# Writing out the sixteen batches of cross attention in place of a loop over pairs

## The chip, the cores and the metric

The kernel runs on one core of a Trainium2 chip. That core has five engines with an instruction stream each: TensorE (PE, matmuls, with its weight loads shown as PEld), VectorE (DVE), ScalarE (ACT), GpSimd (POOL) and SyncE (SP, which only issues DMAs here). They meet only through semaphores. The metric is the device time of one execution in microseconds (us), the median of several runs; lower is better.

## The reference

The model takes x (16 batches x 64 tokens x 256) and a context (16 x 1601 x 192) through six steps, each added to x: cross attention, linear attention, a mixture of experts, a second cross attention with a filter, path attention, and expert-choice experts. The change touches the first alone:

```
def _L0_xattn_ref(x, y, Wq, bq, Wk, bk, Wv, bv, Wo, bo):
    q = _split_heads(x @ Wq + bq)          # 16 heads of 16
    k = _split_heads(y @ Wk + bk)
    v = _split_heads(y @ Wv + bv)
    scores = jnp.einsum('bhqd,bhkd->bhqk', q, k) * scale
    weights = jax.nn.softmax(scores, axis=-1)
    out = jnp.einsum('bhqk,bhkd->bhqd', weights, v)
    out = out.transpose(0, 2, 1, 3).reshape(x.shape[0], x.shape[1], D_ATT)
    return out @ Wo + bo
```

It is called with the layer norm of x and with the context as y. All is in fp32.

## The kernel before

The six steps run one after the other, each in a block of its own in which every engine has its program; the blocks of the other steps have loops of their own. x stays in SBUF.

In `cross_attention` the work goes batch by batch (B = 16, in TILES = 8 pairs, since two batches of 64 tokens fill the 128 partitions). It is a pipeline over two batches: a body for batch n computes its scores, exponentials and weighted sums, and beside that the keys, values and row maxima of batch n + 1. Buffers are double, by h = n mod 2. A body has seven rounds t, each over 256 of the 1601 context rows:

- PE makes the transposed scores of batch n (`scores`, L350), then weighs the values of the round before with its exponentials (`weigh`, L361), then makes a part of the next batch's keys (`keys`, L315) or values (`values`, L322), then direct scores of the next batch for its maximum (`direct`, L331), then another part of keys or values. At the end of a body it spreads the next batch's maximum (`spread_maximum`, L339). The output projection (`project`, L382) comes once in a pair.
- VectorE spreads the queries (L605), subtracts the maximum (L628) and reduces the direct scores (L611, L616).
- ScalarE copies keys and values out of PSUM (L522, L528) and takes exponentials (L536).
- SyncE loads the context of batch b (1.2 MB, L288) when the values of batch b - 2 are made.

Each engine's order is written by hand, and each wait is for a count that grows with the batch. In round 0 of a body, PE's scores stand without a wait of their own ahead of them; in the later rounds they wait for the subtraction and the reduction. On PE, ScalarE and VectorE a helper `batches` (L268) calls the body: batches 0 and 1 are written out, batches 2 to 13 are six passes of a hardware loop whose body holds two batches, and 14 and 15 are written out again. In the loop, n is an expression of the loop's register, and so are the counts waited for and some addresses. SyncE has batches 0 and 1 written out and a loop over the other seven pairs (`first_then_loop`, L31). The engines' loops don't synchronise with each other at their ends; only the semaphores of the work do.

In path attention (`path_attention`) PE runs a loop over the 16 batches as well; its first batch is written out. Its body begins with the matmuls of L2042.

Of the kernel before, what the change touches and what calls it, by code (L numbers as in the profile page):

```python
# [14 lines left out]
B, T, D = 16, 64, 256  # L15
TILES = B * T // P
# [10 lines left out]
def width(c):  # L27
    return P if c < KC - 1 else KLAST


def first_then_loop(eng, count):  # L31

    yield 0
    with eng.Fori(1, count) as i:
        yield i
# [189 lines left out]
def cross_attention(core):  # L225
# [9 lines left out]
    with ExitStack() as stack:  # L235
# [29 lines left out]
        quad = [slice(32 * j, 32 * j + 32) for j in range(4)]  # L265
        block = stack.enter_context(nc.Block())

        def batches(eng, body):  # L268

            body(0, 0, 0, True, False)  # L270
            body(1, 0, 1, False, False)
            with eng.Fori(1, TILES - 1) as i:
                body(2 * i, i, 0, False, False)
                body(2 * i + 1, i, 1, False, False)
            body(B - 2, TILES - 1, 0, False, False)
            body(B - 1, TILES - 1, 1, False, True)

        @block.sync
        def _(sp):
            for dst, name in ((wq, "xa_wq"), (wo, "xa_wo"), (wk, "xa_wk"), (wv, "xa_wv"), (bq, "xa_bq"),  # L280
                              (bk, "xa_bk"), (bv, "xa_bv"), (bo, "xa_bo")):
                sp.dma_start(dst[:], ins[name]).then_inc(w_loaded, 16)
            for i in first_then_loop(sp, TILES):
                for h in range(2):
                    b = 2 * i + h
                    if not isinstance(i, int):
                        sp.wait_ge(v_ps, 7 * (b - 1))
                    sp.dma_start(ctxT[:, h, :, :], ins["ctxT"][ds(b, 1)].rearrange("a k c n -> c (a k) n")  # L288
                                 ).then_inc(ctx_loaded[h], 16)
# [9 lines left out]
        def _(pe):  # L299
# [197 lines left out]
                if not last:  # L497
                    last_maximum(n + 1, 1 - h)

            batches(pe, body)  # L500
            pe.wait_ge(e_done, 7 * B)
            weigh(1, 6)
            pe.wait_ge(oT_ready, 2 * (B - 1))
# [4 lines left out]
        @block.scalar  # L508
        def _(act):
            a_ = nc.scalar.activation  # L510
            ln.scalar(act)
            act.wait_ge(bias_scaled, 1)
            for n in range(2):
                for m in range(KD):
                    act.wait_ge(q_ps, 2 * n + m + 1)
                    a_(qT[:, m, n * 512:(n + 1) * 512], ps[:, 2 * n + m, :], ACT.Identity,
                       bias=bq[:, m:m + 1], scale=DH ** -0.5).then_inc(q_sb, 1)

            def keys_out(b, h, n):
                a, z = PARTS[n // 2]  # L520
                act.wait_ge(k_ps, 8 * b + n + 1)
                a_(kT[:, h, n % 2, a:z], ps[:, KEY_BANK[n], 0:z - a], ACT.Identity, bias=bk[:, n % 2:n % 2 + 1]  # L522
                   ).then_inc(k_sb, 1)

            def values_out(b, h, g):
                w, chunks = width(2 * g), 2 if g < 6 else 1
                act.wait_ge(v_ps, 7 * b + g + 1)
                a_(v[0:w, h, 2 * g:2 * g + chunks].rearrange("p c m d -> p (c m) d")[:, :, 0:16],  # L528
                   ps[0:w, VALUE_BANK[g], 0:chunks * D].rearrange("p (m d) -> p m d", d=16), ACT.Copy).then_inc(v_sb, 1)

            def exponentials(n, h, t):
                w = width(2 * t)
                act.wait_ge(sub_done, 7 * n + t + 1)
                o = probT[0:w, (7 * h + t) % 2].rearrange("p j r c n -> p (j r) c n")
                o = o.rearrange("p u c n -> p (u c n)") if t < 6 else o[:, :, 0, :]
                a_(o, o, ACT.Exp, bias=core.zero[0:w]).then_inc(e_done, 1)  # L536

            def copy_out(b):
                act.wait_ge(pv_done, 7 * b + 7)
                a_(sums_out[:], ps[:, OUT, 0:2 * P], ACT.Copy).then_inc(o_sb, 1)  # L540

            def own_out(b, h):
                act.wait_ge(u_ps, b + 1)
                for e in range(2):
                    a_(oT[:, e, h, :], ps[:, OWN_BANK, e * T:(e + 1) * T], ACT.Identity, bias=bv[:, e:e + 1]).then_inc(oT_ready, 1)

            def spread_out(b):
                act.wait_ge(n_ps, b + 1)
                a_(shift[:].rearrange("p u n -> p (u n)"), ps[:, 5:7, :].rearrange("p b n -> p (b n)"), ACT.Copy
                   ).then_inc(n_sb, 1)  # L550

            def under_shift(b, h, t):
                if t < 4:
                    keys_out(b, h, 2 * t)
                else:
                    values_out(b, h, 2 * (t - 4))

            def under_maximum(b, h, t):
                if t < 4:
                    keys_out(b, h, 2 * t + 1)  # L560
                else:
                    values_out(b, h, 2 * (t - 4) + 1)

            def last_maximum(b, h):
                values_out(b, h, 6)
                spread_out(b)

            for t in range(ROUNDS):
                under_shift(0, 0, t)
                under_maximum(0, 0, t)  # L570
            last_maximum(0, 0)

            def body(n, i, h, first, last):
                for t in range(ROUNDS):
                    if t == 0 and not first:
                        copy_out(n - 1)
                    if t == 3 and not first:
                        own_out(n - 1, 1 - h)
                    if not last:
                        under_shift(n + 1, 1 - h, t)  # L580
                    exponentials(n, h, t)
                    if not last:
                        under_maximum(n + 1, 1 - h, t)
                if not last:
                    last_maximum(n + 1, 1 - h)

            batches(act, body)
            copy_out(B - 1)
            own_out(B - 1, 1)

        @block.vector
        def _(dve):
# [11 lines left out]
            def spread(b, h):  # L604
                v_.tensor_tensor(qb[:, h], qT[:, :, ds(b * T, T)].unsqueeze(2).broadcast_to([P, 2, 2, T]),  # L605
                                 pair_mask[:].unsqueeze(1).unsqueeze(3).broadcast_to([P, 2, 2, T]), ALU.mult).then_inc(qb_ready, 1)

            def reduce(b, n):
                a, z = PARTS[n // 2]
                dve.wait_ge(m_ps, MAXES * b + n + 1)  # L610
                v_.tensor_reduce(part[:, :, n % 2, n // 2], ps[:, 0:4, 0:z - a], AX.X, ALU.max,  # L611
                                 negate=True).then_inc(m_used, 1)

            def maximum(b):
                dve.wait_ge(m_used, MAXES * b + MAXES)
                v_.tensor_reduce(nmax[:], part[:].rearrange("p j r s -> p (j r) s"), AX.X, ALU.min).then_inc(max_step, 1)  # L616

            def subtract(n, h, t, first):

                w, chunks = width(2 * t), 2 if t < 6 else 1  # L620
                dve.wait_ge(s_ps, 7 * n + t + 1)
                if t == 0:
                    dve.wait_ge(n_sb, n + 1)
                if not first or t >= 2:
                    dve.wait_ge(pv_done, 7 * n + t - 1)
                got = ps[0:w, 0:4, :].rearrange("p j (r c n) -> p (j r) c n", r=2, c=2)
                o = probT[0:w, (7 * h + t) % 2].rearrange("p j r c n -> p (j r) c n")
                v_.tensor_tensor(o[:, :, 0:chunks], got[:, :, 0:chunks],  # L628
                                 shift[0:w].unsqueeze(2).broadcast_to([w, 8, chunks, P]), ALU.add).then_inc(sub_done, 1)
# [9 lines left out]
            def add(i):  # L639
                dve.wait_ge(y_ps, i + 1)  # L640
                xt = core.x[:, ds(i, 1), :].rearrange("p a n -> p (a n)")
                v_.tensor_tensor(xt, ps[:, Y_BANK, 0:D], xt, ALU.add).then_inc(x_done, 1)
# [6 lines left out]
            def body(n, i, h, first, last):  # L649
                if not last:  # L650
                    if not first:
                        dve.wait_ge(s_ps, 7 * n)
                    spread(n + 1, 1 - h)
                for t in range(ROUNDS):
                    subtract(n, h, t, first)
                    if not last:
                        reduce(n + 1, t)
                    if t == 1 and not first:
                        normalise(n - 1)
                    if t == 4 and not first and not h:  # L660
                        add(i - 1)
                if not last:
                    reduce(n + 1, 7)
                    maximum(n + 1)

            batches(dve, body)
            normalise(B - 1)
            add(TILES - 1)

# [1942 lines left out]
```

## Time and profile before

| | us |
|---|---|
| median of 3 runs | 3106.34 (3101.46 to 3115.24) |
| the profiled execution, own time | 3107.18 |
| its span, first to last instruction | 3105.4 |
| cross attention's batches in it, about | 76 to 970 |
| PE busy | 2625.1 |
| VectorE busy | 1784.2 |
| ScalarE busy | 1100.4 |
| mean granted clock of PE | 0.915 of full speed |

A row of the timeline is a run of equal instructions with its start, its length, the engine and the line of the code. The list of waits says before which work an engine sat idle and what ended that; "issue" there means that the profile shows nothing that it waited for. The granted clock (PEclk) is 1.00 at full speed and 0.50 at half speed. The DMA queue q8 is one that brings instructions, in packets of 16 KB; q1 brings data.

### The profile page before, as it was taken

What the parts mean: (1) busy time and instruction counts of PE and PEld (TensorE: products, weight loads), DVE (VectorE), ACT (ScalarE), POOL (GpSimd) and SP (SyncE); (2) the same over time, 40 slices, a digit from 0 to 9 for tenths busy, and PEclk for the clock granted to TensorE, in tenths of its full rate; (3) what the DMA queues carried; (4) which work ended last, traced back from release to release, by engine and by line L of the source; (5) the groups of instructions that cost most, each with busy time, mean ns of one, the idle gap of its engine ahead of it and who ended that gap; (6) DMA issues with size and microseconds to landing.
All of it is one profiled execution on the core that took longest, in us unless ns stands there. A gap on an engine that the chain in (4) does not pass through costs nothing. (4 is left out here: it accounts for less than half of the span.)

```text
span 3105.4 us, 80772 instructions
## 1 busy us (share of the span) xinstructions
PE 2625.1 (85%) x34608; PEld 1907.8 (61%) x34608; DVE 1784.2 (57%) x2561; ACT 1100.4 (35%) x1715; POOL 752.6 (24%) x964
## 2 busy tenths in 40 slices
PE   5998988988997899888888868875888888888598
PEld 3565555555564455455655545533888888878487
DVE  4654544545554444399999958158555555655500
ACT  2443433433443111245555531244333323332121
POOL 6900000000000000023333340022556545653200
PEclk9999989999998889999999979987998899899699
DMA  2001001001000011222222210010000000000131
GB/s 72 23 18 33 18 18 34 18 18 34 18 2 22 0 36 35 67 81 82 77 84 74 72 47 1 0 31 4 4 4 3 4 4 4 4 4 3 55 136 41
DMA packets 24546, 99.41 MB, mean 32 GB/s; under 512 B 4825, under 2 KB 9838, under 8 KB 19503
## 3 DMA queue, kind: packets, MB, share of 16 engines
q1 hardware_dynamic: 24238, 94.57, 10.4%
q8 instruction: 284, 4.65, 0.6%
q14 instruction: 24, 0.19, 0.0%
HBM read 93.51 MB, written 1.05 MB: 30 GB/s over the span
## 5 line engine op out<-in xcount | busy, mean ns | idle before, releaser
L611 DVE TENSOR_REDUCE xa_minus_max_parts<-psum 128x4 f32<-128x1600 f32 (+1 forms) x128 | 233.9, 1827 | 220.6 <-PE psum L331 220.6
L628 DVE TENSOR_TENSOR xa_probT<-psum,xa_minus_max_spread 128x2048 f32<-128x2048 f32 (+1 forms) x112 | 239.5, 2139 | 198.1 <-PE psum L350 198.1
L315 PE MATMUL psum<-xa_ctxT,xa_wk 96*128 96x400 f32 (+1 forms) x512 | 217.9, 551 | 2.1 <-DVE xa_qb L605 1.3
L2193 ACT ACTIVATE pa_x<-psum 128x256 f32<-128x256 f32 x256 | 98.1, 383 | 332.0 <-PE psum L2052 316.4
L536 ACT ACTIVATE xa_probT<-xa_probT,zero_column 128x2048 f32<-128x2048 f32 (+1 forms) x112 | 209.4, 1870 | 8.9 <-DVE xa_probT L628 8.9
L322 PE MATMUL psum<-xa_wv,xa_ctxT 96*128 96x256 f32 (+1 forms) x832 | 208.0, 392 | 0.0
L1279 POOL TENSOR_TENSOR tk_exp_all<-tk_exp_all,tk_exp_left 128x577 f32<-128x577 f32 x64 | 120.8, 1888 | 354.5 <-ACT tk_exp_left L1400 354.5
L2017 POOL TENSOR_TENSOR pa_cT<-pa_mt_and_qw,pa_levelT 128x256 f32<-128x256 f32 x256 | 192.3, 784 | 58.6 <-PE psum L2052 58.6
L2271 DVE TENSOR_TENSOR pa_inv_and_invT<-pa_inv_and_invT,psum 128x512 f32<-128x512 f32 x192 | 131.9, 687 | 117.8 <-PE psum L2052 117.6
L716 POOL MEMSET la_v<- 128x512 f32 x1 | 0.5, 524 | 809.9 <-remote 809.9
L350 PE MATMUL psum<-xa_qb,xa_kT 32*128 32x128 f32 (+1 forms) x3328 | 131.8, 295 | 60.8 <-issue 29.2
L322 PEld LDWEIGHTS psum<-xa_wv,xa_ctxT 96*128 96x128 f32 (+1 forms) x832 | 145.7, 185 | 60.7 <-ACT xa_v L528 27.5
L350 PEld LDWEIGHTS psum<-xa_qb,xa_kT 32*128 32x128 f32 (+1 forms) x3328 | 111.5, 194 | 114.7 <-issue 108.8
L1447 DVE MAX8 tk_top<-tk_left 128x8 f32<-128x1601 f32 x96 | 175.1, 1824 | 4.1
L1449 DVE MATCH_REPLACE8 tk_left<-tk_top,tk_left 128x1601 f32<-128x1601 f32 x96 | 173.9, 1811 | 0.0
L2052 PE MATMUL psum<-pa_inv_and_invT,pa_cT 64*64 64x64 f32 x4096 | 144.0, 229 | 28.2 <-DVE pa_prob L2232 24.5
L1352 PE MATMUL psum<-tk_ctx,tk_attnT 128*128 128x192 f32 (+1 forms) x832 | 148.2, 337 | 14.7 <-ACT tk_attnT L1406 14.0
L1332 PE MATMUL psum<-tk_ctxT,tk_qwt 97*128 97x512 f32 (+1 forms) x256 | 128.3, 585 | 36.8 <-ACT tk_ctxT L1422 32.6
L2052 PE MATMUL psum<-pa_inv_and_invT,pa_x 64*64 64x64 f32 x4096 | 157.8, 219 | 0.0
L2052 PEld LDWEIGHTS psum<-pa_inv_and_invT,pa_cT 64*64 64x64 f32 x4096 | 135.2, 143 | 36.3 <-issue 35.7
L1352 PEld LDWEIGHTS psum<-tk_ctx,tk_attnT 128*128 128x128 f32 (+1 forms) x832 | 139.4, 196 | 21.3 <-ACT tk_attnT L1406 21.3
L528 ACT ACTIVATE xa_v<-psum 128x512 f32<-128x512 f32 (+1 forms) x112 | 63.4, 566 | 233.2 <-PE psum L322 233.2
(471 smaller groups left out, 5208.5 us busy)
## 6 DMA issues: line engine op xcount, KB each, us to landing
tk_ctx<-in_ctx SPq DMA_DIRECT2D x16, 1248.0 KB, 5.4
xa_ctxT<-in_ctxT SPq DMA_DIRECT2D x16, 1200.8 KB, 7.4
tk_ctxT<-in_ctxT SPq DMA_DIRECT2D x16, 1200.8 KB
ec_w<-in_ec_w SPq DMA_DIRECT2D x16, 1024.0 KB, 6.8
m_gate_up<-in_m_gate_up SPq DMA_DIRECT2D x17, 256.0 KB, 2.6
m_down<-in_m_down SPq DMA_DIRECT2D x17, 128.0 KB, 2.5
ff_w<-in_ff_w SPq DMA_DIRECT2D x2, 1024.0 KB
x_resident<-in_x SPq DMA_DIRECT2D x1, 1024.0 KB, 4.9
```

The source lines that it names most:

```text
L315: mm = mmul(ps[:, KEY_BANK[n], 0:z - a], wk[:, k, m * P:(m + 1) * P], ctxT[:, h, k, a:z], start=(k == 0), stop=(k == 1))
L322: mm = mmul(ps[0:width(c), VALUE_BANK[g], (c % 2) * D:(c % 2 + 1) * D], ctxT[:, h, k, c * P:c * P + width(c)], wv[:, k, :], start=(k == 0) ...
L350: mm = mmul(ps[0:w, j, (2 * r + c) * P:(2 * r + c + 1) * P], kT[quad[j], h, r, at:at + w], qb[quad[j], h, r, :, :].rearrange("p e t -> p ( ...
L536: a_(o, o, ACT.Exp, bias=core.zero[0:w]).then_inc(e_done, 1)
L611: v_.tensor_reduce(part[:, :, n % 2, n // 2], ps[:, 0:4, 0:z - a], AX.X, ALU.max, negate=True).then_inc(m_used, 1)
L628: v_.tensor_tensor(o[:, :, 0:chunks], got[:, :, 0:chunks], shift[0:w].unsqueeze(2).broadcast_to([w, 8, chunks, P]), ALU.add).then_inc(sub_ ...
L1352: mm = nc.tensor.matmul(flat[:, CCOL:CCOL + C], aT[0:width(c), c, :], ctx[0:width(c), h, c, :], start=(c == KC - 1), stop=(c == 7))
L1447: c.step(nc.vector.max(best, src))
L1449: c.step(nc.vector.match_replace(left[:, u % 2, :], best, src, TAKEN))
L2017: g_.tensor_tensor(cT[:, n % 2, g], mq[:, g, :, 0, :], four(levelT[:, n, :]), ALU.mult).then_inc(level_ready, 1)
L2052: mm = mmul(ps[rows, at, column + j * T:column + (j + 1) * T], left[rows, g, j, :], right[rows, g, j, :], **flags)
L2271: v.tensor_tensor(whole, whole, ps[:, 4 + g, :], ALU.subtract).then_inc(inv_sb, 1)
```

## The change

`batches` is replaced by a plain loop of the program that builds the kernel, so that all sixteen bodies are written out on PE, ScalarE and VectorE, and SyncE's loads likewise. The order of the instructions in a body, the waits, the buffers and the work are the same. The counts and addresses become constants.

```
-        def batches(eng, body):
-
-            body(0, 0, 0, True, False)
-            body(1, 0, 1, False, False)
-            with eng.Fori(1, TILES - 1) as i:
-                body(2 * i, i, 0, False, False)
-                body(2 * i + 1, i, 1, False, False)
-            body(B - 2, TILES - 1, 0, False, False)
-            body(B - 1, TILES - 1, 1, False, True)
+        def batches(body):
+
+            for n in range(B):
+                body(n, n // 2, n % 2, n == 0, n == B - 1)
...
-            for i in first_then_loop(sp, TILES):
+            for i in range(TILES):
                 for h in range(2):
                     b = 2 * i + h
-                    if not isinstance(i, int):
+                    if i:
                         sp.wait_ge(v_ps, 7 * (b - 1))
...
-            batches(pe, body)
+            batches(body)
...
-            batches(act, body)
+            batches(body)
...
-            batches(dve, body)
+            batches(body)
```


## Rows read from the trace of the kernel before

Times are us from the span's start unless marked ns. The waits give us in total, times, longest; a DMA queue row packets, MB, share of the 16 engines. A window's row gives its length, then busy us and count of PE, PEld, DVE, ACT, POOL, then PEclk, DMA share, GB/s. The brackets at the end of a timeline row hold the idle time before it and what released it.

**Rows 1.** the page, busy us (share of the span) x instructions of each engine

```profile
PE 2625.1 (85%) x34608; PEld 1907.8 (61%) x34608; DVE 1784.2 (57%) x2561; ACT 1100.4 (35%) x1715; POOL 752.6 (24%) x964
```

**Rows 2.** who waited for whom, PE, 297 to 885 us: us, times, longest

```profile
PE psum L350 <- issue: 29.2, 5, 6.1
PE psum L350 <- DVE xa_minus_max_parts L611: 15.8, 35, 0.5
```

**Rows 3.** the same view, PE, 184.8 to 291.8 us, whole

```profile
PE psum L350 <- DVE xa_minus_max_parts L611: 3.7, 8, 0.5
PE psum L339 <- DVE xa_minus_max L616: 2.5, 2, 1.3
PE psum L331 <- ACT xa_kT L522: 1.4, 2, 0.7
```

**Rows 4.** timeline (start, us, engine line), PE, boundary of bodies 2 and 3

```profile
237.17 2.02 PE L339 MATMUL psum<-ident,xa_minus_max 128*128 128x128 f32 x16 [1.25 <-DVE xa_minus_max L616]
239.13 1.17 PE L350 MATMUL psum<-xa_qb,xa_kT 32*128 32x128 f32 x32
240.23 0.64 PE L361 MATMUL psum<-xa_probT,xa_v 65*17 65x64 f32 x32
240.80 1.61 PE L315 MATMUL psum<-xa_ctxT,xa_wk 96*128 96x401 f32 x4
243.10 0.96 PE L331 MATMUL psum<-xa_kT,xa_qb 32*128 32x401 f32 x8 [0.69 <-ACT xa_kT L522]
```

**Rows 5.** timeline, all engines, 284 to 302 us, the loop's first jump back

```profile
288.81 0.32 SPq L288 DMA_DIRECT2D xa_ctxT<-in_ctxT  x1
...
289.89 2.02 PE L339 MATMUL psum<-ident,xa_minus_max 128*128 128x128 f32 x16 [1.25 <-DVE xa_minus_max L616]
290.22 0.42 DVE L605 TENSOR_TENSOR xa_qb<-xa_qT,xa_pair_mask 128x256 f32<-128x256 f32 x1 [0.48 <-issue]
...
297.88 2.09 PE L350 MATMUL psum<-xa_qb,xa_kT 32*128 32x128 f32 x32 [5.97 <-issue]
```

**Rows 6.** busy us of each engine, PEclk, DMA by window: straight stretch; behind jump

```profile
88.00:182.00 94.00, 87.65 (x1420) 56.25 (x1407) 57.18 (x32) 40.72 (x45) 67.28 (x75) 1.00 0.06 15
...
297.88:311.84 13.96, 13.27 (x136) 7.82 (x140) 4.56 (x3) 3.46 (x4) 0.00 (x0) 0.50 0.01 2
```

**Rows 7.** the same view for the first, second and last pair of looped bodies

```profile
184.73:291.85 107.12, 99.06 (x1589) 64.05 (x1588) 61.54 (x39) 45.78 (x52) 0.00 (x0) 1.00 0.11 25
297.88:416.73 118.85, 105.49 (x1589) 67.78 (x1589) 61.54 (x39) 45.77 (x52) 0.00 (x0) 0.93 0.10 23
...
770.77:882.91 112.14, 104.59 (x1589) 67.02 (x1589) 61.54 (x39) 44.75 (x51) 0.00 (x0) 0.94 0.06 13
```

**Rows 8.** the same view for body 1, before the loop

```profile
131.93:184.73 52.80, 48.69 (x793) 31.58 (x792) 30.94 (x20) 22.89 (x26) 27.72 (x18) 1.00 0.11 24
```

**Rows 9.** the page, DMA issues: count, KB each, us to landing

```profile
xa_ctxT<-in_ctxT SPq DMA_DIRECT2D x16, 1200.8 KB, 7.4
```

**Rows 10.** DMA queues, instruction packets: 184.73 to 291.85, then 297.88 to 416.73 us

```profile
q8 instruction: 13, 0.21, 0.9%
...
q8 instruction: 14, 0.23, 0.8%
```

**Rows 11.** DMA queues: 288.8 to 294.5, then 294.5 to 297 us

```profile
q1 hardware_dynamic: 178, 1.14, 84.3%
...
q8 instruction: 1, 0.02, 3.3%
```

**Rows 12.** who waited for whom, PE, 2160 to 2880 us

```profile
PE psum L2042 <- issue: 44.9, 14, 3.5
```

**Rows 13.** timeline, SyncE, 232 to 242 us; DMA queues, 242.5 to 245 us

```profile
236.09 0.32 SPq L288 DMA_DIRECT2D xa_ctxT<-in_ctxT  x1
...
q8 instruction: 1, 0.02, 3.0%
```

**Rows 14.** timeline, PE, 79 to 90 us, in body 0

```profile
80.81 1.72 PE L331 MATMUL psum<-xa_kT,xa_qb 32*128 32x401 f32 x8 [0.78 <-ACT xa_kT L522]
```

## Prediction, made before the changed kernel was run

> **What bounds the kernel now.** I read the page first. TensorE (PE) is busy 85% of the span, VectorE 57%, ScalarE 35% [rows 1]. So PE's own stream of instructions sets the pace, and what ends PE's idle times is the question. The list of who waited for whom, for PE from 297 to 885 us, answers it [rows 2]: 29.2 us in 5 waits, up to 6.1 us long, stand at the first score matmul (L350) with no releaser ("issue"), beside 15.8 us in 35 short waits for VectorE's reductions. In the two loop bodies before that (184.8 to 291.8) the "issue" entry is missing altogether; the whole list is three kinds of short waits, 3.7 + 2.5 + 1.4 = 7.6 us [rows 3]. Five is the number of times that a loop of six passes jumps back.
>
> The timeline shows the place. At a boundary between two bodies that are neighbours in the code (237 to 239 us), PE ends the spreading of the maximum (L339), which began at 237.17, and begins the next scores at 239.13, 1.96 us later and with no idle time [rows 4]. At a boundary where the loop jumps back, L339 begins at 289.89 and L350 only at 297.88 [rows 5]: 5.97 us idle. Nothing that this matmul needs is late: the program has no wait before the scores of round 0 and VectorE's last work before it, begun at 290.22 [rows 5], is for the next batch. The other four edges are in the 29.2 us of the list [rows 2].
>
> [...]
>
> **The change, part by part.** (1) The five jumps back go. The cost of a pair of bodies is read as the distance between the first L350 of even batches [rows 5, 7]: with 184.73 and 297.88 the first two, it is 118.85 us from 297.88 to 416.73, and 112.14 for the last pair, from 770.77 to 882.91, which ends without a jump. What a pair takes in straight code is in the trace as well: the first pass is entered without a jump, and its work ends at 289.89 + 1.96 = 291.85, so it takes 291.85 - 184.73 = 107.12 us, at clock 1.00 all through, 99.06 us of it busy [rows 7]. The six passes took 882.91 - 184.73 = 698.18 us, and six straight ones would take 6 x 107.12 = 642.72. The difference is 55.46 us. It splits in the 29.2 us of idle time [rows 2] and a remainder of 26.3 us of slow clock, 5.3 us for each edge. I take both parts as gained: the slow clock stands behind an edge, and in the straight stretches from 88 to 182 and 184.73 to 291.85 it was 1.00 throughout [rows 6, 7], so without the idle time nothing seen here lowers it. What becomes late next is what the straight pair already contains: the waits for VectorE and ScalarE, 7.6 us a pair [rows 3], are inside the 107.12.
>
> (2) The waits and addresses that were computed from the loop's register become constants. Bodies 0, 1, 14 and 15 had constants already. Body 3, with registers, took 52.72 us (from 239.13 [rows 4] to 291.85); body 1, with constants, from 131.93 to 184.73, 52.80 us [rows 8]. So this is worth nothing to within 0.1 us a body, and I take zero; the bounds are -1 and +1 us over twelve bodies. VectorE jumps too, and has an idle time of 0.48 us before its first work behind the jump [rows 5]; that lies under PE's gap and is zero on the path. ScalarE and SyncE jump while they wait for PE anyway. These go at no gain.
>
> (3) SyncE's context transfers keep their order and their waits. Batch b's transfer starts when the values of batch b - 2 are made, and is needed a body (some 53 us) later, against a landing of 7.4 us [rows 9]. Zero.
>
> (4) What is added is code. Ten more bodies lie in line on each engine. Does PE's supply of instructions keep up? The instruction queue of the DMA engines shows it: in the straight pair 13 packets of 16 KB arrive, in a looped pair 14 [rows 10]. The loop's code is brought in anew on every pass, so writing it out brings no more traffic, one packet fewer for each edge. Straight code of this very density (first pass) shows no idle time for it. So zero, with the bounds under the rivals.
>
> Why an edge costs 6 us: the context transfer of 1.2 MB begins at 288.81, just ahead of the jump [rows 5]. From 288.8 to 294.5 only the data queue moves, 178 packets at 84% of the engines; the instruction packet comes in the stretch from 294.5 to 297, and PE starts at 297.88 [rows 11]. In path attention, where nothing is being loaded, PE's idle time at the loop's edges (L2042) is 44.9 us in 14 waits, 3.2 us each [rows 12]. So about 3.2 us are the jump and 2.6 us, the rest of 29.2 / 5 = 5.8, the queueing behind the data. For the sum this doesn't matter, both go; it matters for the first rival.
>
> [...]
>
> The sum: -29.2 - 26.3 = -55.5 us. The profiled execution took 3107.2 us around a span of 3105.4, and the median of the runs shown is 3106.3, so the profile stands 0.8 us above it. 3107.2 - 55.5 = 3051.7 for such an execution, 3050.8 for the median.
>
> **The rivals.** A, slower than before: starved prefetch. In straight code the next instruction packet can also queue behind a context transfer. It seems to: at the boundary of 236 us, where a transfer is issued at 236.09, the next packet of this queue comes in 242.5 to 245 [rows 13]. If PE runs through the block that it holds before that, it idles with 6 us at the worst and then pays the slow clock's 5.3. What protects it is that the stretch under a transfer is thin in instructions: from 236.1 to 243.1 PE runs 16 + 32 + 32 + 4 matmuls [rows 4], each with one weight load, 168 instructions, and a packet of 16 KB carries more: 13 packets serve 1589 matmuls and 1588 loads [rows 7, 10], over 240 in each. The boundary at 236 shows it without idle time. But the straight code meets some ten more transfers, each at a place in its block not sampled so far. Lost at all ten, 8 us each (2.6 of queueing and 5.3 of clock, as above), that is 80 us: 3051 + 80 = 3131. It decides from 5.5 us on average over the ten. Against it speaks that about 70 instructions are to spare; chance 0.04.
>
> B: the later loops move. The code of the following stages begins elsewhere in its 16 KB blocks. If the target of path attention's jump comes to lie near a block's end, PE runs into a second fetch: up to 2 us more at each of 14 edges, since 32 matmuls with their loads take 1.2 to 2.1 us [rows 4, 5] against the 3.2 us of a jump's fetch. 28 us more: 3079. One or two missed prefetches of A are worth as much. It can also go the other way, if fewer of these 14 edges are followed by the slow clock: half a microsecond or so at each with the matmuls of [rows 4, 5], under 10 us in all, 3041. Chance of a loss of 15 to 35 us: 0.09.
>
> C: the idle time goes but the clock doesn't gain. If the clock falls of itself some time in long dense runs, the 26.3 us stay: 3077. For it: in the first written-out body, without a jump, the eight matmuls at 80.81 us take 1.72 us, where those at 243.10 take 0.96, behind an idle time of 0.78 [rows 14, 4]. Against it: 94 and 107 us at 1.00 [rows 6, 7]. Chance 0.04.
>
> D: the gap isn't the jump but the transfer, or the change does nothing to it: 3106. The boundary at 236 us has the same transfer (issued at 236.09) and no gap [rows 13, 4], which nearly excludes it. Chance 0.03.
>
> **How the numbers follow.** Forecast, 3035 to 3066 us: 0.80. B 0.09, C 0.04, D 0.03, A 0.04. Predicted 3051. The range of 8 in 10 reaches down by B's possible gain with the runs' own spread (3040; these went from 3101.5 to 3115.2), and up over the lighter half of B (3070). About 0.5%, or 15.5 us, is what a measurement of this kernel can tell from no change: faster than that are the forecast, B, C: 0.93; I give 0.92 for faster, 0.05 for the same (D, and part of A), and 0.03 for slower.
>
> **What would show it.** PE's wait list should have no "issue" of over 1 us at L350; pairs of bodies should be 107.1 us apart from first to last; granted clock 1.00 from 88 us to the end of cross attention; batch 14's first L350 at 184.7 + 642.7 = 827.4 instead of 882.9 us. The edges in path attention should still stand at about 3.2 us, 14 times. Wrong would be: "issue" idle times of 2 to 6 us on PE at new places, just behind the start of a context transfer (A); longer ones at L2042 (B); slices of clock 0.5 within cross attention with no idle time before them (C).

## The result

The changed kernel takes 3083.99 us (median of 8 runs, 3076.17 to 3096.16) against 3114.82 (3095.28 to 3126.99) for the kernel before: ratio 0.990, with an interval of 0.9875 to 0.9925. It is faster by 31 us, about 1%; the forecast was 55 us, and the range of 3040 to 3070 missed the time. Its profiled execution took 3081.99 us with a span of 3080.4, 25.0 us under the span of before.

The first stage did what was forecast. Three windows of pairs of bodies in the changed kernel, the last one ending at batch 14's first L345 (L350 before); columns as in [rows 6, 7]:

```profile
184.92:292.19 107.27, 99.05 (x1591) 64.13 (x1590) 61.36 (x39) 45.77 (x52) 0.00 (x0) 1.00 0.10 25
292.19:399.46 107.27, 99.05 (x1591) 64.12 (x1590) 61.35 (x39) 45.78 (x52) 0.00 (x0) 1.00 0.11 25
...
721.26:828.53 107.27, 99.05 (x1591) 64.12 (x1590) 61.36 (x39) 45.78 (x52) 0.00 (x0) 1.00 0.08 20
```

Each pair takes 107.27 us at full clock, where looped ones took up to 118.85 [rows 7]. Who waited for whom, PE, 60 to 980 us of the changed kernel, longest in total first:

```profile
PE psum L345 <- DVE xa_minus_max_parts L606: 27.0, 59, 0.5
PE psum L334 <- DVE xa_minus_max L611: 20.0, 16, 1.3
PE psum L326 <- ACT xa_kT L517: 11.7, 15, 0.8
PE psum L164 <- DVE la_ln_xn L155: 5.8, 1, 5.8
```

The 29.2 us without a releaser [rows 2] are gone. The first transposes of linear attention (L164) start at 919.37 us in the changed kernel and at 975.64 before: 56.3 us earlier.

The rest came back later. Two windows of each kernel, linear attention and the stretch of path attention from its first to its last moving matmul; first before, then after:

```profile
975.64:1096.38 120.74, 99.41 (x352) 56.08 (x352) 53.78 (x116) 25.38 (x45) 2.64 (x6) 0.80 0.03 9
2155.60:2821.50 665.90, 575.75 (x16168) 557.25 (x16172) 370.53 (x608) 224.44 (x519) 373.37 (x497) 0.91 0.02 4
```

```profile
919.37:1046.10 126.73, 105.25 (x353) 59.30 (x353) 53.77 (x116) 25.46 (x45) 2.64 (x6) 0.76 0.03 9
2101.70:2793.60 691.90, 603.19 (x16174) 578.68 (x16174) 377.57 (x610) 224.35 (x519) 373.51 (x499) 0.87 0.02 4
```

Path attention's stretch is 26.0 us longer with the same work, at a mean clock of 0.87 in place of 0.91. All of it is busy time, 603.19 us against 575.75; the rest of the stretch, in which PE sits idle, went from 90.2 to 88.7 us. Linear attention is 6.0 us longer, with the same count of work and a lower clock. All other stages together are 0.7 us shorter: 56.3 - 26.0 - 6.0 + 0.7 = 25.0.

In path attention the waits without a releaser rose, and those for VectorE fell. From PE's list for 2095 to 2810 us of the changed kernel (its L2037 is L2042 of [rows 12]), and, last, the line of before that answers its third:

```profile
PE psum L2037 <- issue: 61.9, 25, 4.3
...
PE psum L2047 <- issue: 6.0, 17, 0.6
...
PE psum L2065 <- DVE pa_mt_and_qw L2252: 1.4, 1, 1.4
```

```profile
PE psum L2070 <- DVE pa_mt_and_qw L2257: 16.4, 14, 1.7
```

The first was 44.9 us in 14 waits [rows 12] and is 61.9 in 25; the third was 16.4 us and is 1.4. The timeline of one edge shows one of the eleven extra waits:

```profile
2231.97 2.09 PE L2037 MATMUL psum<-pa_moving,pa_wt 32*128 32x128 f32 x32 [4.29 <-issue]
2233.84 0.65 PE L2037 MATMUL psum<-pa_moving,pa_wbt 32*128 32x128 f32 x7
2235.17 1.86 PE L2037 MATMUL psum<-pa_moving,pa_wbt 32*128 32x128 f32 x25 [0.68 <-issue]
```

PE stops in the middle of a group of equal matmuls, after 32 + 7 = 39 of them, which no semaphore explains. All eleven stand at this matmul. The view of one source line holds the jump itself, on PE's sequencer. Lowest, median and highest duration in ns; first the line of path attention's loop, then that of cross attention's, both before, then path attention's after:

```profile
L2149 PEldq COMPARE_BRANCH  x15: 83/3671/3887, 2234.7 to 2861.3; - x15
```

```profile
L272 PEldq COMPARE_BRANCH  x6: 83/7558/7784, 290.1 to 881.1; - x6
```

```profile
L2144 PEldq COMPARE_BRANCH  x15: 83/4208/4662, 2180.6 to 2832.1; - x15
```

The 83 ns are the last pass, where the jump isn't taken. Path attention's jumps went from 3.67 to 4.21 us though nothing in its loop was edited. What did change is where it lies: ten more bodies of code stand ahead of it. That is rival B, to which the prediction gave 0.09.

### The profile page after: what moved, and what is told of

It is laid out like the page before. It is cut to its first block and busy times, and to the rows that moved or that the text cites. A ratio compares the mean times of both kernels' runs of the same rounds, so it can differ in the third digit from the quotient of the medians.

```text
span 3080.4 us, 79974 instructions
## 1 busy us (share of the span) xinstructions
PE 2628.9 (85%) x34608; PEld 1915.9 (62%) x34608; DVE 1789.2 (58%) x2561; ACT 1100.4 (36%) x1715; POOL 751.2 (24%) x964
## 5 line engine op out<-in xcount | busy, mean ns | idle before, releaser
L310 PE MATMUL psum<-xa_ctxT,xa_wk 96*128 96x400 f32 (+1 forms) x512 | 204.0, 521 | 2.2 <-DVE xa_qb L600 1.3
L2047 PE MATMUL psum<-pa_inv_and_invT,pa_cT 64*64 64x64 f32 x4096 | 142.6, 227 | 19.7 <-DVE pa_prob L2227 16.1
L345 PEld LDWEIGHTS psum<-xa_qb,xa_kT 32*128 32x128 f32 (+1 forms) x3328 | 105.4, 184 | 86.0 <-issue 78.9
L345 PE MATMUL psum<-xa_qb,xa_kT 32*128 32x128 f32 (+1 forms) x3328 | 125.1, 285 | 34.4 <-DVE xa_minus_max_parts L606 27.0
L2047 PEld LDWEIGHTS psum<-pa_inv_and_invT,pa_cT 64*64 64x64 f32 x4096 | 133.8, 142 | 28.0 <-issue 27.4
```

Of the source, the lines that this page charges most:

```text
L310: mm = mmul(ps[:, KEY_BANK[n], 0:z - a], wk[:, k, m * P:(m + 1) * P], ctxT[:, h, k, a:z], start=(k == 0), stop=(k == 1))
L345: mm = mmul(ps[0:w, j, (2 * r + c) * P:(2 * r + c + 1) * P], kT[quad[j], h, r, at:at + w], qb[quad[j], h, r, :, :].rearrange("p e t -> p ( ...
L2047: mm = mmul(ps[rows, at, column + j * T:column + (j + 1) * T], left[rows, g, j, :], right[rows, g, j, :], **flags)
```

## The experiments

Two questions: is it the place of path attention's loop that cost 26 us, and what did the edges in cross attention really cost? PE's code comes in the 16 KB packets of q8. Over the straight code of cross attention in the changed kernel (90 to 880 us) PE runs 256.1 instructions from one packet to the next on average (92 packets), so a fetch block of 16 KB is taken as 256 instructions. A helper of the language places a loop's first instruction at a chosen one of them. "Place s" below means s instructions lie ahead of the target in its block.

**Places 0 and 224, in the changed kernel.**

```
-                with pe.Fori(1, B) as b:
+                with nc.Fori(1, B, engines=bass.OrderedEngineSet([pe.engine]), head_slot={pe.engine: 0}) as b:
```

> The changed kernel, with one edit: PE's loop in path attention is placed so that its first instruction is the first of a 16 KB fetch block (256 instructions); the padding before it is jumped over once. Theory 1 (the loss of 26 us in path attention comes from where the loop now lies in its blocks: about 83 instructions of the block are left behind the jump's target, PE then runs dry, and a prefetch is in flight when it jumps): the second idle time behind each jump goes, the jumps take some 3.6 us instead of 4.2, the stretch from path attention's first moving matmul to the last is back at about 666 us from 692, and the whole at about 3058 us. Theory 2 (the loss has nothing to do with the place, but with the clock after a denser first stage or with this execution): the stretch stays at 692 us and the whole at 3082.

Measured 3062.72 us (3053.97 to 3072.81), ratio 0.9828 (0.9793 to 0.9863). The jumps are back at 3.5 us and no second wait follows one, but the profiled execution, the slowest of the four, had a stretch of 685.6 us. PE's waits without a releaser in that stretch:

```profile
PE psum L2037 <- issue: 45.6, 15, 3.4
...
PE psum L2047 <- issue: 17.9, 30, 1.2
```

The first line is as before the change; the second, the waits within the body, was 2.9 us there. So theory 1 holds for the edges and misses 15 us of waits in the body.

> The changed kernel, with PE's loop in path attention placed 32 instructions before the end of a fetch block. Theory 1 (place): PE runs out after some 16 matmuls behind each of the 14 jumps and waits for 2 to 3 us for the next block, so there are 14 more waits of that size than in the well placed loop; the stretch takes 695 to 720 us and the whole 3085 to 3110 us, no gain over the kernel before. Theory 2 (not the place): 692 us and 3082, as in the changed kernel.

Measured 3102.66 us (3091.31 to 3108.22), ratio 0.9972 (0.9953 to 0.9991): theory 1. The timeline counts the instructions that were left:

```profile
2226.63 1.23 PE L2037 MATMUL psum<-pa_moving,pa_wt 32*128 32x128 f32 x15 [3.56 <-issue]
2229.56 1.43 PE L2037 MATMUL psum<-pa_moving,pa_wt 32*128 32x128 f32 x17 [1.70 <-issue]
```

Fifteen matmuls with their loads and two register instructions are 32; then PE waits 1.7 us. It is out of code: the second packet of q8 behind this jump ends at 2228.3 us, and PE goes on 1.3 us after that. By the same count the changed kernel has 82 or 83 left, 39 matmuls with their loads and four register instructions, so its loop lies at about place 173.

**Place 173, in the kernel before.**

```
-                with pe.Fori(1, B) as b:
+                with nc.Fori(1, B, engines=bass.OrderedEngineSet([pe.engine]), head_slot={pe.engine: 173}) as b:
```

> The kernel before, with its loop in cross attention, and with PE's loop in path attention placed at instruction 173 of its fetch block, so that 83 are left behind the jump's target: the place read for the changed kernel from the 39 matmuls that run before its second wait. Nothing else differs. Theory 1 (what the change lost in path attention is the place alone): the stretch goes from 666 to about 692 us, with jumps of 4.2 us and a second wait of 0.4 to 0.7 us behind most, and the whole to about 3133. Theory 2 (it was something that writing out cross attention did to the stages behind it): 666 us and 3107.

Measured 3144.06 us (3136.08 to 3164.28) against 3114.24, ratio 1.0091 (1.0061 to 1.0121). The kernel before, with its first stage untouched, loses 30 us by this alone. Its stretch and its jumps:

```profile
2163.60:2866.30 702.70, 603.12 (x16170) 578.14 (x16173) 383.56 (x610) 224.78 (x519) 373.35 (x500) 0.88 0.02 4
```

```profile
L2149 PEldq COMPARE_BRANCH  x16: 83/4196/4534, 2200.9 to 2905.4; - x16
```

Jumps of 4.2 us, and the matmuls split 7 + 25 again (the sixteenth branch, here and below, enters the loop over the padding). The stretch is 11 us longer than forecast; that the place causes the loss is settled by it. Of the 36.8 us by which the stretch grew, 27.4 are busy time (603.12 against 575.75 us). This kernel also took 130.7 us in linear attention, whose code and surroundings are those of before, where it was 120.7. So the 6 us there need not be the change's: over all the profiled executions here that stage takes anything from 119 to 131 us.

**Places 16, 64 and 128, in the changed kernel** (the same edit with another number).

> The changed kernel, with PE's loop in path attention at instruction 16 of its fetch block. In the kernel before, the last packet ahead of each jump comes 1.2 to 1.4 us before it; with the loop at instruction 0 it comes 0.5 to 0.8 before, in the changed kernel at the jump. If the place in the block is all, then at 16 the block that holds the jump is entered earlier by 240 to 250 instructions, the waits within the body fall from 18.8 us towards the 2.9 us of the kernel before, the stretch takes 666 to 672 us, and the whole 3055. If the waits within the body were only that one execution, it is the same as with the loop at instruction 0: 3062, within what the runs spread.

Measured 3055.67 us (3055.17 to 3058.94), ratio 0.9828 (0.9802 to 0.9855). The waits in the body are 4.7 us, and the stretch is 665.3 us, that of the kernel before. (At place 0 the last packet sets out 0.4 to 1.0 us ahead of the jump, not 0.5 to 0.8.)

> The same with the loop at instruction 64: 192 instructions are left behind the target, enough for the 64 matmuls of the first two groups (128 instructions) before the next block is needed. By the place: no second wait behind the jumps; the jump itself stands 41 instructions into a block, so a packet is on its way when it is taken and the jumps take about 4.2 us in place of 3.5: 14 x 0.7 = 10 us more than at instruction 0, the whole 3065 to 3075. By a theory in which only the rest of the target's block counts: 3055 to 3062, no dearer than at 0.

Measured 3069.40 us (3060.76 to 3096.82), ratio 0.9871 (0.9839 to 0.9902), stretch 682.3. The whole is where it was expected, but not by that mechanism: the jumps took 3.4 us, not 4.2, and PE's idle time in the stretch is no longer than at place 16 (85.1 against 87.6 us). The 17 us between the two stretches are busy time again, at a clock of 0.88 against 0.91. The ten runs at place 64 spread over 36 us, so that the clock of this one says little of the place.

> The same with the loop at instruction 128: 128 are left behind the target, of which the first 64 matmuls take all but a few. By the place: the second block is asked for when PE resumes and is there 2.8 us later (read in the changed kernel: 2232.4 to 2235.2), while 128 instructions take PE 2.1 us at full and 3.8 us at half clock, so short second waits, under 0.7 us, at some of the edges; the whole 3062 to 3080, between 0 and 173.

Measured 3086.49 us (3077.54 to 3089.07), ratio 0.9915 (0.9885 to 0.9945), stretch 701.9: over the upper end of what was expected, and again otherwise. There was no second wait; it was the jumps that grew. Their rows at 16, 64 and 128:

```profile
L2144 PEldq COMPARE_BRANCH  x16: 83/3529/3883, 2140.9 to 2807.5; - x16
```

```profile
L2144 PEldq COMPARE_BRANCH  x16: 83/3402/3685, 2140.6 to 2826.1; - x16
```

```profile
L2144 PEldq COMPARE_BRANCH  x16: 83/4708/4922, 2136.6 to 2841.5; - x16
```

So two things depend on the place: how much of the target's block is left, and when, seen from the jump, the last packet of straight code sets out. The packets of q8 in the traces show what the second does. Medians over the 14 jumps back, in us; times are counted from the start of the jump:

| place | last straight packet starts | target's packet starts | it takes | jump |
|---|---|---|---|---|
| 64 | -2.5 | 1.0 | 1.0 | 3.4 |
| kernel before | -1.3 | 1.0 | 1.0 | 3.7 |
| 16 | -1.2 | 1.0 | 1.1 | 3.5 |
| 0 | -0.9 | 1.0 | 1.1 | 3.5 |
| 224 | -0.5 | 1.0 | 1.4 | 3.8 |
| changed kernel, about 173 | 0.0 | 1.0 | 1.8 | 4.2 |
| 128 | 0.6 | 1.0 | 1.9 | 4.7 |

The target's packet sets out at the same time everywhere, but takes nearly twice as long where a packet of straight code set out at most 1.0 us before it, and the jumps there are the longest. No run took the straight packet away alone, so that the one slows the other is argued, from seven places that fall in line. Medians of the whole by place (0, 16, 64, 128, the changed kernel at about 173, 224): 3062.7, 3055.7, 3069.4, 3086.5, 3084.0, 3102.7 us: 47 us between the best and the worst place of one loop. Places 0 and 16 can't be told apart (both have the ratio 0.9828).

**The transfer moved behind the jump, in the kernel before.**

```
-                        sp.wait_ge(v_ps, 7 * (b - 1))
+                        sp.wait_ge(s_ps, 7 * (b - 2) + 1)
```

> The kernel before, with the context transfer of batch b issued not when the values of batch b - 2 are made, just ahead of the jump, but when the first scores of the body of batch b - 2 are, just behind it. Theory 1 (an edge is some 3.2 us of fetch and 2.6 us of queueing behind the transfer): the five jumps fall from 7.6 us to about 5, PE's idle time at L350 from 29.2 us to about 16, and the whole by 13 us or a little more, to about 3093. Theory 2 (the transfer is no part of it): the jumps stay at 7.1 to 7.8 us and the whole at 3107. In either case the transfer is still done some 40 us before it is needed.

Measured 3078.99 us (3068.54 to 3086.52), ratio 0.9878 (0.9839 to 0.9916). One line, the loop kept, and the gain is as large as that of the change. The jumps, and the whole of cross attention in one window:

```profile
L272 PEldq COMPARE_BRANCH  x6: 83/3698/3814, 287.6 to 833.5; - x6
```

```profile
88.00:900.00 812.00, 739.75 (x11969) 480.86 (x11964) 461.86 (x291) 343.28 (x387) 67.28 (x75) 1.00 0.09 22
```

The timeline of its first edge shows what is left of it:

```profile
287.42 2.02 PE L339 MATMUL psum<-ident,xa_minus_max 128*128 128x128 f32 x16 [1.25 <-DVE xa_minus_max L616]
...
291.50 1.17 PE L350 MATMUL psum<-xa_qb,xa_kT 32*128 32x128 f32 x32 [2.05 <-issue]
...
292.86 0.32 SPq L288 DMA_DIRECT2D xa_ctxT<-in_ctxT  x1
```

A jump takes 3.7 us instead of 7.6: the target's packet sets out 1.0 us behind its start, where it was 4.5 to 5.1 us in the kernel before with the transfer ahead. 1.7 us of the jump lie under the work that PE has queued; the idle time is 2.05 us, and behind it the 32 matmuls take 1.17 us, at full clock. Cross attention takes 898.1 us from its first transposes to those of the next stage, instead of 945.8: of the 56 us that writing it out brings there, 48 were the transfer's. Theory 1 holds, but its sizes were too small (jumps of 5 us, 13 us on the whole): the queueing was 3.9 us a jump, and in this execution the slow clock went with the shorter gap (not wholly in another, below).

**The target named ahead, in either kernel.**

```
-            with eng.Fori(1, TILES - 1) as i:
+            with nc.Fori(1, TILES - 1, engines=bass.OrderedEngineSet([eng.engine]), hint_back_edge=eng.engine == mybir.EngineType.PE) as i:
```

This adds one instruction at the head of PE's loop, 0.04 us long in the trace, that names the target of the loop's jump.

> The kernel before, loop and all, with the same kind of instruction at the head of PE's loop over pairs of batches in cross attention; nothing is written out. Theory 1 (fetch of the target): the five jumps of 7.1 to 7.8 us go under 0.5, the slow clock behind them goes, pairs are 107 us apart, and the whole is 3107 - 55 = about 3052 us, since path attention's loop keeps its place but for one or two instructions (3045 to 3062). Theory 2 (written-out code is needed): no more than 10 us below the kernel before.

Measured 3055.74 us (3051.39 to 3057.63), ratio 0.9812 (0.9781 to 0.9843):

```profile
L272 PEldq COMPARE_BRANCH  x6: 88/364/407, 288.7 to 824.3; - x6
```

The jumps take 0.36 us and cross attention 888.0 us, against 889.6 when written out. That is theory 1. The packets of q8 show that the target's block comes before the jump here. A pass has 13 of them, against 14 in the kernel before and with the transfer moved. None sets out 1.0 us behind the jump, nor anywhere from 8.2 us ahead of it to 4.6 us behind it, and yet PE runs the target's code after 0.36 us. The packet that sets out about 8.5 us ahead (8.2 to 8.6) is the target's, then, and not that of the code that follows the loop: in the last pass, in which the jump isn't taken, that code comes by a packet of its own 1.3 us behind the branch, where the kernel before needs none until 3.3 us behind it.

So the edges were all there was to gain in this stage: neither the constants nor straight code bring anything beyond them, to within these 1.6 us. The same in path attention's loop of the changed kernel:

```
-                with pe.Fori(1, B) as b:
+                with nc.Fori(1, B, engines=bass.OrderedEngineSet([pe.engine]), hint_back_edge=True) as b:
```

> The changed kernel, with one instruction at the head of PE's loop in path attention that names the target of the loop's jump ahead of time, so that its block can be fetched before the jump. Theory 1 (a jump costs the fetch of its target): the 14 jumps fall from 4.2 us to under 0.5, their second waits go, and PE's clock falls less often: 14 x 3.8 + 7 = 60 us and 10 to 30 more, the whole at about 2995 us (2980 to 3020). Theory 2 (a jump costs an emptying of the engine, whatever is fetched): within 5 us of 3082.

Measured 3053.66 us (3052.53 to 3062.00), ratio 0.9816 (0.9783 to 0.9849). This is a miss: the jumps fell only to 2.5 us, and waits in the body stayed (10.2 us). It gains 30 us, not 87. With the loop at place 0 as well (`head_slot={pe.engine: 0}` beside the hint):

> The changed kernel, with PE's loop in path attention placed at the start of a fetch block and the jump's target named at its head. With 83 instructions left in the block and the target named, the jumps took 2.5 us, and second waits came behind them. If the rest of that was the block running out, the jumps now fall under 1 us with no second wait, and the whole goes to about 3020 us. If naming the target only hides part of a fetch wherever the loop lies, the jumps stay at about 2.5 us and the whole comes to 3045.

Measured 3052.05 us (3046.19 to 3065.27), ratio 0.9794 (0.9749 to 0.9839), jumps of 1.55 us. Neither expectation holds. The packets of q8 show what does. In both runs a pass has one packet fewer than without the instruction (10 against 11, and 9 against 10), and none sets out 1.0 us behind the jump. The last one until PE goes on sets out 0.1 us behind the jump's start in the first run and 0.9 us ahead of it in the second, as the last straight packet does in the same loops without the instruction (the table above), and each of the 28 jumps back ends 1.35 to 1.53 us behind the end of that packet. Without the instruction a jump ends 1.4 us in the median behind the end of the target's own packet (1.8 us at place 128). So the named target came in place of the last straight packet, and a jump is hidden as far as that packet is early: 8.5 us ahead of the jump in cross attention's loop, at the jump or 0.9 us ahead of it in this one. That it is the target's is read from times and counts; the trace doesn't tell what a packet holds.

**Path attention written out on PE.**

```
-                with pe.Fori(1, B) as b:
+                for b in range(1, B):
                     batch(b, False)
```

> The changed kernel, with PE's part of path attention written out for its fifteen batches too; the other engines keep their loops there. Theory 1 (a jump of PE to a block that it doesn't hold costs 3 to 4 us of idle time and the slow clock behind it): 61.9 us of idle time go, and 10 to 30 us of slow clock; the stretch takes 600 to 630 us and the whole about 3000. Theory 2 (the dense body outruns the supply of instructions once there are no jumps, so that the time comes back as waits within the bodies): the waits without a releaser in this stretch stay over 40 us, and the whole above 3050.

Measured 3001.87 us (2998.09 to 3005.88), ratio 0.9618 (0.9581 to 0.9655), the fastest kernel here. PE's waits in the stretch, now 613.3 us long:

```profile
PE psum L2047 <- DVE pa_prob L2227: 30.8, 14, 2.7
PE psum L2065 <- DVE pa_mt_and_qw L2252: 25.9, 15, 1.8
...
PE psum L2047 <- issue: 1.5, 5, 0.3
PE psum L2037 <- issue: 0.2, 1, 0.2
```

Of 68 us without a releaser 1.7 are left. Straight code of this body, with some 53 matmuls and weight loads a us (30 in cross attention's), doesn't outrun its supply; VectorE's waits grow in their place (the first was 16.1 us in the changed kernel, the second 1.4). Theory 1 holds. And in the kernel before, with cross attention's loop kept, the transfer late and path attention written out on PE:

> The kernel before with its loop over pairs in cross attention kept, the context transfer issued behind the first scores of batch b - 2, and PE's part of path attention written out. Theory 1 (the edges were dear for the queueing and the slow clock behind a long gap, and the rest is in path attention's edges): cross attention takes 10 us more than when written out, path attention the same 613 us, the whole about 3010. Theory 2 (written-out cross attention brings something else): 3025 or more.

Measured 3020.29 us (3015.27 to 3029.08), ratio 0.9714 (0.9682 to 0.9747). That lies between the two theories' numbers. Path attention took 610.9 us, cross attention 906.1, that is 18 us more than in the kernel with both written out, not 10. Half of the 18 are five idle times at the edges, 9.1 us in all as the list of waits has it; the other half goes with slow clock, which came back behind two of them. The fourth edge:

```profile
622.88 1.86 PE L350 MATMUL psum<-xa_qb,xa_kT 32*128 32x128 f32 x32 [2.12 <-issue]
```

```profile
622.88:634.00 11.12, 10.44 (x88) 5.47 (x92) 4.12 (x2) 3.02 (x4) 0.00 (x0) 0.54 0.49 112
```

The first edge was followed by half clock as well (0.73 from 293.5 to 306 us), the other three by none. So with the transfer out of the way a gap of about 2 us was followed by half clock at two edges of ten, over both executions. What decides it stays open.

## Why the prediction was wrong, point by point

- What bounds cross attention, and the five edges: right. The idle time and the slow clock both went (the granted clock is 1.00 from 88 to 886 us, and 0.86 over the last 33 us of the stage, so rival C stayed away too); 107.12 us a pair was forecast, 107.27 measured; 827.4 us for batch 14's first scores was forecast, 828.5 measured; 55.5 us of gain was forecast and 56.3 are there at the stage's end.
- Registers and constants at zero: right, by the loop with its target named, which is as fast as the written-out code. The context transfers at zero: right too, since the straight code shows no wait for them.
- The added code at zero: this is the step that failed. It was right for the stage itself (rival A stayed away: no wait without a releaser in cross attention) and wrong for the stages behind. The sum had no term for them; measured, they took back 26.0 us in path attention. They stood only in rival B, with 28 us and a chance of 0.09. The range then reached only over "the lighter half of B". The kernel's other long loop, of which PE's trace has some 2,260 instructions a pass, was at a good place before: its jumps, its waits in the body and its 665.9 us are close to those of place 16. The change moved it by a count that I didn't work out. In the programs as built the loop begins 16,019 instructions later than before, 147 further on in a block of 256, so it was at about place 26. From a good place most moves lose: against 16, the places 64, 128, 173 and 224 lose 14 to 47 us, and place 0 can't be told from it. A chance of one half for a loss of 10 to 45 us would have been fair, and the range should have reached to 3100.
- That B's 28 us are near the 26.0 measured is luck: its mechanism was one second fetch of up to 2 us at each of 14 edges. Measured, the 17.0 us more of idle time at L2037 are two terms: 9.6 us in the 14 waits behind the jumps, which B didn't have (44.9 to 54.6 us), and 7.4 us in eleven second waits. And this idle time isn't what the stretch lost: PE's waits for VectorE became 20.6 us shorter (16.4 to 1.4 and 21.7 to 16.1), so that its idle time as a whole stayed where it was, and the 26.0 us are busy time, with the mean clock at 0.87 in place of 0.91. The loss of this execution thus goes with the slow clock; that the longer and split gaps bring it on is argued, not shown. B priced no clock in its loss, only in its possible gain. At place 128 it was otherwise: 26 us more idle time than at 16, and 10 of busy time.
- The split of an edge in 3.2 us of fetch and 2.6 us of queueing was right on the jump (7.6 to 3.7 us without the transfer, so the queueing is even 3.9), and wrong where it said that it matters only for the first rival. The queueing did much to decide whether the clock fell: behind all five edges with it, behind two of ten without it. Had I followed it, a cheaper edit with the same gain was in sight.
- The branch's own duration stood in the trace of before, in the view of its source line (the two rows above). I read only the idle time behind it. It tells the cost of a jump directly, and for small loops too: those with 146 to 505 instructions a pass in PE's trace show a median of 0.21 us.

```profile
L34 PEldq COMPARE_BRANCH  x20: 76/208/244, 1021.6 to 3056.3; - x20
```

- The median of before was put at 3106.3; eight runs gave 3114.8. That moves the forecast by 8 us and doesn't account for the miss: with the loop at place 16 the changed kernel has the forecast gain, 3110.58 - 3055.67 = 54.9 us.

## What to carry to other kernels

The code that this change added moved the loops behind it; path attention's lies 147 of 256 instructions further on. Where a loop is long (here 2,260 and 3,256 instructions a pass on PE paid, 146 to 505 did not), look up the durations of its branches and whether a wait without a releaser splits a group of equal matmuls, and give the stages behind a term of the sum; better, place the loop, or write it out too. And look at what is issued just ahead of a jump: a large transfer there cost more than the jump itself (3.9 against 3.7 us), and may be free to start a little later.

## What the runs showed of the hardware

- The jump back of PE's long loops takes 3.4 to 4.7 us by the place of the loop in path attention (medians of seven places), 3.4 to 3.7 us in cross attention with the transfer moved, 7.6 us there behind a transfer of 1.2 MB that keeps the DMA engines 84% busy, and 0.2 us in loops of up to 505 instructions. On VectorE and ScalarE the jumps of cross attention's loop take 0.04 to 0.07 us.
- A packet of instructions that is fetched for a jump sets out 1.0 us behind the jump's start (0.9 to 1.6 over all jumps), and the jump ends 1.4 us behind the packet's end (1.8 at place 128). The packet takes 0.9 to 1.3 us in the median of a run where the last packet of straight code set out 1.9 us or more before it, and 1.8 to 1.9 us where that was 0.4 to 1.0 us before it; behind the start of a 1.2 MB transfer it sets out only after 4.5 to 5.1 us.
- With the jump's target named at the loop's head there is one packet fewer a pass and none at 1.0 us. Jumps take 0.36 us where the last packet ahead set out 8.5 us before the jump, 1.55 us where it set out 0.9 us before, and 2.5 us where it set out at the jump.
- Idle times of 5.4 to 6.1 us in cross attention were each followed by half clock, 5.3 us of loss on average; with the transfer moved, of ten idle times of 1.6 to 2.1 us in two executions, eight were followed by none (all five of one execution, with a clock of 1.00 over 812 us) and two by 7 and 10 us of half clock.
- Written out, the code of path attention's body, 53 matmuls and weight loads a us, comes in as fast as PE runs it: 1.7 us of waits without a releaser in 613 us.
